# Giving ScalarE three of the four quarter counts in a threshold search (gated MLP with a low-rank mixture layer, 8 cores)

## The reference

```python
def _L0_attn_ref(x, w_gate, w_up, w_down):
    s = silu(einsum('bsh,ih->bsi', x, w_gate))      # I = 11008
    k = int(0.5 * I)
    _, idx = top_k(-abs(s), k)                      # the k smallest |s| of each row
    s = s with 0 at idx
    s = s * einsum('bsh,ih->bsi', x, w_up)
    return einsum('bsi,hi->bsh', s, w_down)

x = x + layernorm(_L0_attn_ref(layernorm(x), w_gate, w_up, w_down))
x = x + layernorm(_L0_ffn_ref(layernorm(x), W, b, Wq, Wk, A, Bm))
```

## Time and profile before

| | |
|---|---|
| median of 2 runs | 9256.36 us (9251.26 to 9261.47) |
| the profiled execution, its own time | 9243.26 us |
| its span, first to last instruction, on the slowest core (core 1) | 9241.7 us |
| spans of the other cores | 9202.1 to 9237.6 us |
| TensorE / VectorE / ScalarE busy, share of the span | 51% / 25% / 32% |
| Sign passes of ScalarE in the search (line 528) | 320, 828.1 us busy |
| counts of VectorE in the search (line 516) | 320, 985.3 us busy |

### The profile page before, as it was taken

The page is one execution under the profiler, slowest core; times in us unless marked ns, Lnnn a source line. Parts: engine busy times, 40 slices in busy tenths (PEclk is TensorE's granted clock), DMA queues, the critical chain, the costliest instruction groups (busy, mean ns, idle before and its releaser), DMA issues.

```text
span 9241.7 us, 59714 instructions; the slowest of 8 cores (9202.1 to 9241.7 us)
## 1 busy us (share of the span) xinstructions
PE 4707.4 (51%) x20664; PEld 2043.7 (22%) x20664; DVE 2285.2 (25%) x4971; ACT 2960.6 (32%) x3864; POOL 319.9 (3%) x611
## 2 busy tenths in 40 slices
PE   2888200004766788717528881000056767888175
PEld 1333100001322333303213330000022323333032
DVE  0000677873011000010100007777821010000101
ACT  6110544453333200062160115444533332000621
POOL 0000000000000000000000000000000000000000
PEclk9999655556888899958759995555578888999587
DMA  2666100002444566615416661000034444666144
GB/s 64 123 123 121 34 0 0 0 0 55 87 83 86 96 120 121 119 34 95 115 56 125 123 118 29 0 0 0 0 60 86 87 83 91 114 121 119 38 93 103
DMA packets 90760, 674.95 MB, mean 73 GB/s; under 512 B 10064, under 2 KB 10080, under 8 KB 14176
## 3 DMA queue, kind: packets, MB, share of 16 engines
q0 software_dynamic: 87008, 620.80, 36.2%
q1 hardware_dynamic: 3456, 50.33, 1.4%
HBM read 1275.08 MB, written 16.78 MB: 140 GB/s over the span
## 4 chain that ended last, share of the span: by engine, by line
PE 35%; ACT 20%; DMA 18%; issue 13%; DVE 13%; DVEq 1%; ACTq 0%; POOLq 0%; SPq 0%
PE pA L373 20%; ACT scr L528 9%; PE pA L645 8%; DMA wslot<-wd 7%; DMA wslot<-wg 5%; PE pA L909 4%; DMA wslot<-wu 4%; ACT L528 2%; PE pT L218 2%; DMA wslot<-wW 2%; DVE scr L570 1%; DVE scr L587 1%; DVE stat L591 1%; DVE stat L464 1%; ACT L230 1%
## 5 line engine op out<-in xcount | busy, mean ns | idle before, releaser
L373 PE MATMUL pA<-wslot,xlT 128*128 128x512 f16 (+1 forms) x11264 | 2569.8, 389 | 345.8 <-DMA wslot<-wg 125.8
L218 PE MATMUL pT<-ident,scr 128*128 128x128 f16 x1200 | 255.7, 261 | 3693.8 <-DVE scr L426 2397.8
L373 PEld LDWEIGHTS pA<-wslot,xlT 128*128 128x128 f16 x11264 | 1119.2, 101 | 1778.1 <-issue 636.6
L645 PE MATMUL pA<-wslot,s 128*128 128x512 f16 x5504 | 1267.8, 390 | 235.5 <-DMA wslot<-wd 156.4
L230 ACT ACT_TABLE_LOAD x608 | 780.1, 1283 | 1458.5 <-PE pT L218 1458.5
L516 DVE TENSOR_SCALAR_CACHE_REDUCE scr<-u,stat 128x2752 f16<-128x2752 f16 x320 | 985.3, 3079 | 42.8 <-DVE stat L510 2.4
L218 PEld LDWEIGHTS pT<-ident,scr 128*128 128x128 f16 x1200 | 123.9, 104 | 3839.2 <-issue 3802.1
L528 ACT ACTIVATE scr<-u,stat 128x2752 f16<-128x2752 f16 x320 | 828.1, 2588 | 17.2 <-ACT scr L528 0.7
L645 PEld LDWEIGHTS pA<-wslot,s 128*128 128x128 f16 x5504 | 538.8, 100 | 964.0 <-issue 378.6
L421 DVE SCALAR_TENSOR_TENSOR scr<-scr,stat,s 128x512 f16<-128x512 f16 (+1 forms) x176 | 129.3, 735 | 1795.3 <-PE pA L373 1795.3
L909 PE MATMUL pA<-wslot,xlT 128*128 128x512 f16 x2048 | 495.4, 401 | 125.3 <-ACT scr L943 75.0
(11 more groups left out here) (132 smaller groups left out, 2494.8 us busy)
## 6 DMA issues: line engine op xcount, KB each, us to landing
wslot<-wg POOLq DMA_DIRECT2D x168, 1024.0 KB, 8.7
wslot<-wu POOLq DMA_DIRECT2D x168, 1024.0 KB, 8.3
wslot<-wd POOLq DMA_DIRECT2D x160, 1024.0 KB, 8.4
wslot<-wW POOLq DMA_DIRECT2D x64, 1024.0 KB, 7.8
xtile<-x SPq DMA_DIRECT2D x16, 2048.0 KB, 7.9
out<-xtile SPq DMA_DIRECT2D x8, 2048.0 KB, 6.9
wslot<-wd POOLq DMA_DIRECT2D x16, 768.0 KB, 7.4
wslot<-wqk POOLq DMA_DIRECT2D x8, 1024.0 KB, 12.2
```

The source lines that it names most:

```text
L218: ins = t.transpose(pT[:, off:off + 128], srcap, ident[:])
L373: ins = t.matmul(pA[:, tt * 512:tt * 512 + wd], xlT[:, (c * nt + tt) * 128:(c * nt + tt) * 128 + 128], wslot[sl][:, ci * wd:(ci + 1) * wd] ...
L645: ins = t.matmul(pA[:, tt * 512:tt * 512 + 512], s_t[tt][:, ic * 128:(ic + 1) * 128], wslot[sl][:, ci * 512:(ci + 1) * 512], start=(ic == ...
```

## The change

In each iteration quarter 1 goes from VectorE to ScalarE: VectorE counts quarter 0 alone, ScalarE takes the signs over quarters 1, 2 and 3. The merge is rewritten for three sums of signs over 3 x 2752 elements; its four instructions each wait for the one before. All else is as it was.

```diff
-                    for qq in range(2):
-                        ins = v.tensor_scalar(dmp, u_sb[:, qq * Qh:(qq + 1) * Qh],
-                                              st("m"), None,
-                                              op0=ALU.is_le, op1=ALU.add,
-                                              accum_out=st("cq1", qq))
-                        t6 = C.inc(ins, ch_v, 1)
-                        C.wait(v, "v", ch_v, t6)
+                    ins = v.tensor_scalar(dmp, u_sb[:, 0:Qh],
+                                          st("m"), None,
+                                          op0=ALU.is_le, op1=ALU.add,
+                                          accum_out=st("cq1", 0))
+                    t6 = C.inc(ins, ch_v, 1)
+                    C.wait(v, "v", ch_v, t6)
...
-                    for qq in (2, 3):
+                    for qq in (1, 2, 3):
                         ins = s.activation(dmp2, u_sb[:, qq * Qh:(qq + 1) * Qh],
                                            ACTF.Sign, bias=st("m"), scale=-1.0,
-                                           accum_out=st("sg", qq - 2))
+                                           accum_out=st("sg", qq - 1))
...
                     C.wait(v, "v", ch_s, toksl[("actc", it)])
-                    v.tensor_add(st("t1"), st("cq1", 0), st("cq1", 1))
-                    ins = v.tensor_add(st("t2"), st("sg", 0), st("sg", 1))
+                    ins = v.tensor_add(st("t1"), st("sg", 0), st("sg", 1))
                     t0 = C.inc(ins, ch_v, 1)
                     C.wait(v, "v", ch_v, t0)
-                    ins = v.tensor_scalar(st("t2"), st("t2"), 0.5, float(Qh),
-                                          op0=ALU.mult, op1=ALU.add)
+                    ins = v.tensor_add(st("t1"), st("t1"), st("sg", 2))
                     t1 = C.inc(ins, ch_v, 1)
                     C.wait(v, "v", ch_v, t1)
-                    ins = v.tensor_add(st("cnt"), st("t1"), st("t2"))
+                    ins = v.tensor_scalar(st("t1"), st("t1"), 0.5,
+                                          1.5 * float(Qh),
+                                          op0=ALU.mult, op1=ALU.add)
                     t2 = C.inc(ins, ch_v, 1)
                     C.wait(v, "v", ch_v, t2)
+                    ins = v.tensor_add(st("cnt"), st("t1"), st("cq1", 0))
+                    t2c = C.inc(ins, ch_v, 1)
+                    C.wait(v, "v", ch_v, t2c)
```

## The result

| | before | changed |
|---|---|---|
| ratio of the times | 1 | 1.0505, 95% interval 1.0453 to 1.0557 |
| median of all runs of the comparison | 9324.35 us (10 runs, 9251.26 to 9528.12) | 9927.91 us (11 runs, 9716.74 to 10068.24) |
| the profiled execution, its own time | 9243.26 us | 9734.21 us |
| its span, slowest core | 9241.7 us (core 1) | 9732.6 us (core 1) |
| Sign passes on ScalarE: number, busy | 320, 828.1 us | 480, 1242.2 us |

The change makes the kernel slower by 5%. The medians of all runs lie above the profiled executions, and 9927.91 above my range, because in six of the changed kernel's 11 executions (and, by their times, probably in some of before's) the cores of one or both dies ran at a lower granted clock (0.69 to 0.72 where the profiled one has 0.75) and the execution took 194 to 334 us more; the ratio leaves those out.

A forecast was written before the change was run, and what follows sets the result against it. The prediction took the threshold search to bound the kernel, with ScalarE the later engine in its count. Third pass 444.0 plus merge 28.8 gave 472.8 us; with 9243.26 and 13.1 that made 9729 us, range 9700 to 9755.

The forecast's parts named there:

- What bounds an iteration: Threshold search: of the count alone ScalarE, with its table load, is later than VectorE by 0.40 us; period 11.54 us.
- (a): Search loop, VectorE: losing its second count of 3.21 us is worth 0 us and lengthens its wait.
- (b): Search loop, ScalarE: a third pass costs 2.775 us from start to start, 444.0 us over 160 iterations.
- (c): Merge on VectorE: four linked instructions take 1.04 us instead of 0.86, adding 0.18 us, 28.8 us over 160 iterations.
- The sum: Search loop: 2.775 + 0.18 = 2.955 us per iteration, 472.8 us over 160, profiled execution 9716.1 us.
- TensorE's longest wait: Up stage, a sign to check: the longest wait grows from 1157 by 236 to 1394 us.
- The step that failed: Whole kernel: the median's 13.1 us above the profiled execution stays, giving 9729 us; shown runs spread over 10 us.
- R1: ScalarE in the search: passes overlap, the third costs 2.51 us, 430 us in all, time 9687; chance 0.04.
- R2: Search: ScalarE is slow because VectorE reads the same tile; lone passes get shorter, 9284 at half price; chance 0.02.
- R3: Stages after the search: longer rest gives TensorE a higher granted clock, winning 72 us, time 9657; chance 0.01.
- R4: Search loop: costlier hand-offs, 3.24 us per iteration, 518 us in all, time 9775; chance 0.02.
- R5: Search loop: the change does not do what it says; no chance beyond a rounding.

The follow-up runs named there:

- experiment 4: Kernel before, VectorE's count of quarter 1 left out, first sum added twice instead: 0.00 us per iteration; median 9373.96 us beside 9363.21, no verdict.
- experiment 5: Changed kernel with a one-column Sign ahead of ScalarE's wait, so the table load comes early: 1.29 us less per iteration; ratio 1.027 against before.
- experiment 6: Kernel before, 2:2 split kept, with ScalarE's table load brought ahead of its wait for the guess: -0.31 us per iteration, ratio 0.9923.
- experiment 3: Kernel before, both VectorE counts kept, plus a third ScalarE pass over quarter 1 whose sum is unused: +2.78 us per iteration, ratio 1.0459.
- experiment 2: Changed kernel with the merge's first two instructions a pair again, so only the third pass is added: +2.78 us per iteration, ratio 1.0458 against before.
- experiment 8: Changed kernel, ScalarE's second pass given its own output tile and no wait for the first: +2.56 us per iteration against before; median 9732.53 us, no verdict.
- experiment 1: Kernel before, only the merge changed so that its two first adds each wait: +0.20 us per iteration; median 9465.23 us beside 9363.21, no verdict.

## Why the prediction was right, and where it was wrong

The mechanism held, and the loop's price came out within 4 us of the measured 477; the stated range did not hold the median of all runs.

**What bounds an iteration** (ScalarE, by 0.4 us, with VectorE close behind). Right: experiment 4 takes VectorE's count away for nothing, experiment 5 gets the whole of ScalarE's table load back, and experiment 6 only 0.31 us of it.

**(a), VectorE's relief is worth 0.** Right, by experiments 3 and 4 (2.78 with and without it; 0.00 alone).

**(b), 2.775 us for the third pass.** Measured 2.78 in experiments 2 and 3. Taking it from start to start, and not from the instruction's 2.588 us, was worth 0.19 us or 30 us in all, and experiment 8 shows that it is not in the read-out: it goes with the wait for the pass before and the output tile that the two share.

**(c), 0.18 us for the merge.** Measured 0.20 (experiment 1). I counted the links at 0.26 us each and they are 0.26 to 0.27; 3 us in all.

**The sum.** 2.955 us per iteration forecast, 2.98 measured; 472.8 us against 476.8. The profiled execution was to take 9716.1 us and took 9734.2; of the 18 us 4 are the loop's, and 14 lie outside the search, where profiles of kernels with equal code there differ by up to 88 us (experiments' introduction). The other signs came as forecast: VectorE's idle time before the merge is 1039.7 us in all where I had put 1040, and TensorE's longest wait 1397.1 us where I had put 1394.

**The step that failed** is the last one, "the difference has nothing to do with the loop, so it stays: 9716.1 + 13.1 = 9729 us", with the range made from runs that "spread over 10 us". Two runs do not show the spread of this program. In the comparison, the median of before itself is 9324.35 us, 81 above its profiled execution and not 13, and the changed kernel's is 194 above its own. By the ratio the forecast holds, 1.0505 x 9256.4 = 9724 us beside 9729, but the median of all runs, 9927.91 us, lies outside the 9700 to 9755. The term between profiled execution and median was right in having nothing to do with the loop and wrong in being a constant. The traces show where such time lies: in experiment 4's execution cores 0 to 3 had a mean granted clock of 0.75 and cores 4 to 7 one of 0.765, the search stretches agree within 2 us (2350.1 to 2351.6 us together), and outside the search the former took 6958 us on average and the latter 6885. So 73 us went with 0.014 of TensorE's mean clock, all of it outside the search. Why the clock is lower in some executions, and whether the change makes that more frequent, was not tried and stays open.

**The rivals.** R1 (passes overlap, 2.51 us) did not happen; with the wait and the shared output tile removed the distance is 2.575, so there was 0.20 and not 0.27 us to be had. The 2.51 us of the earlier trace rows was no distance between two passes either: what follows the Abs pass there is a table load. R2 (ScalarE slow beside VectorE): out, by experiment 3. R3 (a higher granted clock after the rest): out; up has 0.81 again, and 587.00 / 2500 = 0.235 us per matmul. Its price for a full clock, 72 us, was probably too small, since in experiment 4 a mean clock lower by only 0.014 already went with 73 us. R4 (costlier hand-offs): out; the merge starts 0.10 us after the read-out though VectorE has waited 6.5 us. R5 (not the change it says): out, with 480 passes and 160 counts.

## What to carry to other kernels

Where two engines share a step and then meet, lay out one period in order of time and read which one the meeting point waited for; busy totals over the stretch pointed at the other engine here (939 us against 580), because they count the serial part too. Price moved work on the receiving engine from start to start of its neighbours, waits and read-outs included, and price the relief of an engine by who is late: nothing if the meeting point waits for the other engine (experiments 3 and 4), and at most the margin by which the relieved engine is late otherwise (experiment 6: 0.31 us for 1.28 us taken off). And before moving work, look at what else the late engine does inside the shared step: here a table load of 1.28 us and a chain of waits could be moved out, which together with a split by speed gave 1.7% where moving a quarter cost 5%.

## What I had not expected of the hardware

- A wait of ScalarE for its own previous pass looks free, since the two passes stand one behind the other anyway. With it and one output tile for both the starts lie 2.775 us apart, without it and with two tiles 2.575 us (experiment 8). On VectorE the same kind of wait, put between two one-column instructions and nothing else changed, cost 0.20 us per iteration (experiment 1).
- The table load costs 1.28 us and the pass follows 0.01 us behind it (1097.27 + 1.28 to 1098.56 in the earlier trace rows). The Trainium skill, "ScalarE: Activation LUTs", section "What ACT_TABLE_LOAD costs", adds a drain of 1.38 us for a switch between sets; no such time shows here, where each section loads ahead of a Sign after a Sign.
- Within VectorE, 0.17 us of idle time stand between the read-out of a count and the instruction that waits for it in the next section, against 0.10 from ScalarE's read-out to the merge, so the margin between two engines is smaller than the difference of their ends (0.31 us for 0.40, experiment 6).
